# Taking the 64x64 inverse of a delta-rule block from a transpose on TensorE instead of from 32x32 products

## What is computed

```
sk = einsum('bhij,bhj->bhi', St, k_)
err = sk - v_
Sn = a_ * St - b_ * err[..., None] * k_[..., None, :]
o_ = einsum('bhij,bhj->bhi', Sn, q_)
```

## Time and profile before

| | us |
|---|---|
| median of 3 runs | 2829.43 (2828.09 to 2830.31) |
| the profiled execution | 2829.43 |
| its span | 2827.4 |
| TensorE busy | 2742.5 |
| VectorE busy | 1754.5 |
| ScalarE busy | 1222.6 |
| GpSimd busy | 607.1 |

### The profile page before, as it was taken

One profiled execution on the slowest core, in us unless ns is written; L12 is line 12 of the kernel. 1 busy time (PEld: TensorE's weight loads), 2 busy tenths in 40 slices (PEclk: granted clock), 3 DMA queues, 4 the chain that ended last, 5 costly groups with the idle time before them and its releaser, 6 DMA issues. The chain is left out here.

```text
span 2827.4 us, 38098 instructions
## 1 busy us (share of the span) xinstructions
PE 2742.5 (97%) x13297; PEld 1540.9 (54%) x13298; DVE 1754.5 (62%) x4334; ACT 1222.6 (43%) x2268; POOL 607.1 (21%) x670
## 2 busy tenths in 40 slices
PE   8999999989999988999999999999999999999998
PEld 3444444445566445665666656666566665664432
DVE  5867762011111176778877788777877778645986
ACT  4646441011211145456545565555645555342243
POOL 2111101401111312132133321333213331120000
PEclk9999999999999988999999999999999999999999
DMA  3101124031112562011100112001120011227313
GB/s 135 51 1 45 45 104 192 20 123 66 61 65 67 211 244 79 16 42 65 75 31 31 43 55 85 31 31 43 50 85 32 35 39 52 75 76 268 122 49 105
DMA packets 78503, 215.25 MB, mean 76 GB/s; under 512 B 12128, under 2 KB 13056, under 8 KB 69760
## 3 DMA queue, kind: packets, MB, share of 16 engines
q1 hardware_dynamic: 58704, 165.84, 16.2%
q0 software_dynamic: 9264, 28.36, 3.1%
q10 hardware_dynamic: 10368, 18.88, 1.8%
HBM read 156.25 MB, written 56.80 MB: 75 GB/s over the span
## 5 line engine op out<-in xcount | busy, mean ns | idle before, releaser
L2469 DVE SCALAR_TENSOR_TENSOR c_conv<-c_ps_pj,c_conv_t,c_conv 128x511 f32<-128x511 f32 (+2 forms) x450 | 336.0, 747 | 33.4 <-ACT c_conv L2288 22.8
L1962 POOL TENSOR_SCALAR c_gate<-c_gate 128x512 f32<-128x512 f32 x64 | 37.8, 618 | 980.5 <-DVE c_block_L L2502 980.5
L2038 PE MATMUL c_ps_pj<-c_xs,c_w_v 128*128 128x512 f32 x480 | 225.8, 593 | 0.0
L2038 PE MATMUL c_ps_pj<-c_xs,c_w_q 128*128 128x512 f32 x360 | 173.0, 610 | 0.0
L2059 PE MATMUL c_ps_pj<-c_w_g,c_xs 128*128 128x512 f32 x384 | 172.7, 592 | 0.0
L2038 PE MATMUL c_ps_pj<-c_xs,c_w_k 128*128 128x512 f32 x360 | 164.4, 593 | 0.0
L1284 DVE TENSOR_TENSOR x_act<-x_hs,x_ps_u 128x352 f32<-128x352 f32 x40 | 20.8, 521 | 191.5 <-ACT x_hs L1269 191.5
L2288 ACT ACTIVATE c_conv<-c_ps_pj,c_conv_t 128x512 f32<-128x512 f32 x150 | 116.3, 776 | 48.9 <-issue 27.4
L2351 ACT ACTIVATE c_err<-c_negL 32x128 f32<-32x128 f32 x256 | 78.6, 307 | 134.0 <-DVE c_negL L2535 129.3
L2499 DVE TENSOR_TENSOR c_block_X<-c_block_X,c_block_t 128x58 f32<-128x58 f32 (+6 forms) x448 | 117.7, 263 | 15.4
L2496 DVE TENSOR_TENSOR c_block_t<-c_block_L,c_block_X 128x58 f32<-128x58 f32 (+6 forms) x448 | 117.6, 262 | 14.9
(11 more groups left out here) (585 smaller groups left out, 5951.4 us busy)
## 6 DMA issues: line engine op xcount, KB each, us to landing
c_xs<-xt_d SPq DMA_DIRECT2D x16, 1024.0 KB, 4.8
c_G<-cum_d SPq DMA_DIRECT2D x16, 1024.0 KB, 4.7
ot_d<-c_oT ACTq DMA_DIRECT2D x64, 256.0 KB, 2.0
b_w_gu<-in_w_gu SPq DMA_DIRECT2D x8, 1408.0 KB, 21.5
y_slots<-x_y SPq DMA_DIRECT2D x40, 256.0 KB, 2.0
d_x<-x SPq DMA_DIRECT2D x32, 256.0 KB
d_switch<-in_switch_w SPq DMA_DIRECT2D x4, 2048.0 KB, 17.1
a_x<-in_x SPq DMA_DIRECT2D x7, 1024.0 KB, 7.3
```

The costliest lines, as they stand in the source:

```text
L2038: mm = e.matmul(bank_of[xb][u][:, :], w["kqv"[u // HG]][:, k, (u % HG) * DH:(u % HG + 1) * DH], xs[xb][:, k, :], start=(k == 0), stop=(k = ...
L2469: e.scalar_tensor_tensor(oc, bank_of[buf][u][:, 0:SEQ - s], conv_t[buf][:, m, h, TAPS - 1 - s:TAPS - s], oc, ALU.mult, ALU.add).then_inc(c ...
```

## The change

T's upper 64x64 is no longer put together from two spread blocks, a cleared block and a product. It is got in one piece as the transpose of R's upper 64x64, once that is whole.

- Gone: the 16 matmuls of L2167, T's spread 1 and the copy L2402 on ScalarE, and one clearing of a block of T on GpSimd at the phase's start.
- New on TensorE: `turn_inverse(p)`, eight transposes for each pair of chunks. The stationary operand is R's upper 64 rows by 128 columns, the moving one a 64x64 identity, so the output is 128 partitions by 64 columns, in `t_ps` for p = 0 and in `d_ps` for p = 1. They wait for both copies of R's off-diagonal blocks (`rl_done`, `rb_done`), for all spreads of R, and for the last copy of v (`v_done`), which `r_blocks` waited for before.
- New on ScalarE: two copies of 64x512, PSUM to T, behind the tap of unit HG+2.
- Order on TensorE: `r_blocks`, half of HG+2, **both `turn_inverse`**, half of HG+3, `z_half(0)`, a **quarter** of HG+3, `z_half(1)` with `r_half(0)`, the other **quarter**, `r_half(1)`. `z_half(p)` waits for the copy of T of its own pair.

```diff
-                e.memset(T[even_of[0], :, :, odd_of[0]], 0.0).then_inc(cleared, 1)
...
-                    e.wait_ge(T_done, 3 * r + 2)
+                    e.wait_ge(T_done, 2 * (r + 1))
...
-                    e.wait_ge(v_done, r * TPB + TPB)
...
-                            mm = e.matmul(t_block[odd_of[0], c, h, :], R[odd_of[0], c, h, odd_of[0]], Z[odd_of[0], c, h, even_of[0]],
-                                          start=True, stop=True)
-                            if c == TPB - 1 and h == HG - 1:
-                                mm.then_inc(tl_ready, 1)
...
+                def turn_inverse(p):
+
+                    if p == 0:
+                        e.wait_ge(v_done, r * TPB + TPB)
+                        e.wait_ge(R_done, TPB * r + TPB)
+                        e.wait_ge(rl_done, 3 * r + 1)
+                        e.wait_ge(rb_done, r + 1)
+                    for c in (2 * p, 2 * p + 1):
+                        for h in range(HG):
+                            mm = e.transpose(t_pair[p][:, c % 2, h, :], R[upper_half, c, h, :], con["ident"][upper_half, upper_half])
+                    mm.then_inc(tl_ready, 1)
+
+                def next_quarter(u, k):
+                    if not last:
+                        unit(r + 1, 1 - buf, u, (k // 2,), 16 * half + 16, ks=(k,))
+                        return
+                    h = (u + 1) * HG + k
+                    out_part(h // NH, (h % NH,))
...
-                    if i == 0 and p == 0:
-                        if not after_first(r):
-                            e.wait_ge(cleared, 3)
-                        e.wait_ge(T_done, 3 * r + 3)
-                        e.wait_ge(tl_done, r + 1)
+                    if i == 0:
+                        e.wait_ge(tl_done, PAIRS * r + p + 1)
...
                 next_unit(HG + 2, (1,))
+                for p in range(PAIRS):
+                    turn_inverse(p)
+                next_unit(HG + 3, (0,))
                 for i in range(2 * HG):
                     z_half(0, i)
-                next_unit(HG + 3, (0,))
+                next_quarter(HG + 3, 2)
                 for i in range(2 * HG):
                     z_half(1, i)
                     r_half(0, i)
-                next_unit(HG + 3, (1,))
+                next_quarter(HG + 3, 3)
...
-                spread(T, corner_T, 1, T_done)
                 next_silu(HG - 1)
-                e.wait_ge(tl_ready, r + 1)
-                e.activation(T[odd_of[0], :, :, even_of[0]], t_block[odd_of[0]], ACT.Copy).then_inc(tl_done, 1)
                 e.wait_ge(rl_ready, 4 * r + 2)
                 e.activation(R[even_of[1], :, :, odd_of[1]], r_block[1][even_of[1]], ACT.Copy).then_inc(rb_done, 1)
                 next_tap(HG + 2)
...
+                for p in range(PAIRS):
+                    e.wait_ge(tl_ready, PAIRS * r + p + 1)
+                    e.activation(T[upper_half, 2 * p:2 * p + 2, :, upper_half], t_pair[p][upper_half], ACT.Copy).then_inc(tl_done, 1)
```

More of the change, by code:

```diff
@@ L1802, in phase_delta @@
         z_block, r_block = [by_block(z_ps), by_block(d_ps)], [by_block(r_ps), by_block(kk_ps)]
-        t_block = by_block(t_ps)
-        z_pair, r_pair = [by_pair(z_ps), by_pair(d_ps)], [by_pair(r_ps), by_pair(kk_ps)]
+        z_pair, r_pair, t_pair = [by_pair(z_ps), by_pair(d_ps)], [by_pair(r_ps), by_pair(kk_ps)], [by_pair(t_ps), by_pair(d_ps)]
         even_of = [slice(2 * BB * b, 2 * BB * b + BB) for b in range(2)]
@@ L2190, in r_half @@
                     if i == 0:
[L2191 to L2194, removed]
                         e.wait_ge(zl_done, 4 * r + 3 + p)
```

## The result

The changed kernel took 2847.65 us in the median (2841.21 to 2849.38, 5 runs), the kernel before beside it 2828.39 us. The ratio of the means is 1.0062 with a 95% interval of 1.0047 to 1.0077: 0.6% slower, 17.5 us, with an interval of 13.3 to 21.8 us. The interval holds that, and it also holds the 20.9 us of the rival with 0.083 us per transpose: the total alone does not tell them apart, the rounds do. The profiled execution took 2848.35 us.

The account below looks back on a forecast made before the run. The prediction took TensorE to bound the kernel: 16 x 1.27 = 20.3 us added, 15 x 0.33 = 5.0 removed, r_blocks 0, so 2829.4 + 15.3 = 2844.7 us, range 2838 to 2857.

Parts of the forecast that it names:

- the rival with 0.083 us per transpose: New transposes take 0.083 us each, not 0.061: 2850.3 us in all; chance 0.13 together with the 0.109 case.
- TensorE sets the round: Attention rounds last as long as TensorE's work plus one wait of 0.3 us; TensorE time enters the span one to one.
- The third tile is free: In r_blocks, removing the 16 matmuls of L2167 saves 0.00 us, at most 0.01, since three tiles run side by side.
- The wait costs 0.33 us: First matmul of z_half(0) waits for ScalarE's copy of T; the new order removes 0.33 us in 15 rounds, 5.0 us.
- The turn block takes 1.27 us: The 16 new transposes on TensorE: 0.98 us plus 0.29 for changes of shape, in all 16 rounds, 20.3 us added.
- the slower-transpose rival: New transposes take 0.083 us each (2850.3 us) or 0.109 (2857.0 us), not 0.061; chance 0.13 for the two together.
- No new wait, thin cover: At r_half, a quarter of HG+3 covers ScalarE's copy of Z with 0.22 us margin, where 1.08 was; cost zero.
- The sum: Per execution: 20.3 us added, 5.0 removed, r_blocks 0; net +15.3 us, giving 2844.7 us, 0.5% slower.

Follow-up runs that it names:

- two_tiles: The kernel before without the 16 matmuls of L2167, ScalarE's copy waiting for the L2172 matmuls instead: ratio to before 0.9999.
- copy_first: The kernel before with ScalarE's copy of T (L2402) moved ahead of the silu: ratio to before 0.9982, 5.1 us faster.
- order_only: The kernel before with only the new TensorE order of HG+3's half and quarters, T made as before, no transposes: ratio to before 0.9980.
- no_cover: The changed kernel with both quarters of HG+3 ahead of z_half(1) and r_half(0), none ahead of r_half(1): ratio to before 1.0070.
- extra_turn: order_only plus 16 transposes of negL, result unused, ahead of the half of HG+3: ratio to before 1.0061.
- adjacent: order_only plus 16 transposes of negL, placed directly ahead of z_half(0): ratio to before 1.0048.

## Why the prediction was right

- *TensorE sets the round.* Right: the changed kernel's TensorE is busy for 89.89 of 89.89 us, and the turn block's 1.33 us less the wait's 0.33 are the 1.00 by which the round grew.
- *The third tile is free.* Right: 0.00 us in two_tiles. By a count of instructions the sum would have been 5.4 us smaller.
- *The wait costs 0.33 us.* Right: 88.89 to 88.56 in copy_first and order_only, 15 rounds, 5.0 us.
- *The turn block takes 1.27 us.* Right in kind, mis-sized by 0.06: it takes 1.33. The transpose was put at 0.061 and takes 0.0625; the changes of shape were put at 0.29, from the four transposes of L952, and take 0.33. That the 64 streamed and the 128 loaded columns would cost hardly more than either alone held. Neither the 0.083 nor the 0.109 of the slower-transpose rival is there. The loads of the new transposes, from the trace of the changed kernel, and those of the 128x128 ones, from that of the kernel before:

```profile
L2178 PEld LDWEIGHTS c_ps_t<-ident,c_R x128: 134/138/142, 1155.8 to 2512.4; 64*128 64x128 f32 x128
...
L2137 PEld LDWEIGHTS c_ps_t<-ident,c_vT x256: 139/141/142, 1129.4 to 2481.3; 128*128 128x128 f32 x128
```

  A load record lasts 138 ns here, 136 in L952 and 141 in the 128x128 transposes, though these stand 109 ns apart and the others 61 and 62.5. So the length of the record does not tell what a transpose costs, the distance between starts does. The 128 loaded columns are common to all three, so they don't set the 109; whether the 128 rows or the 128 streamed columns do, no run shows. The Trainium skill (TensorE: Matmul & The Clock Gate, LDWEIGHTS (loading the stationary operand)) gives a load of 128 columns 107 ns, by columns / 1.2. Neither the 62.5 ns between the new transposes nor the 138 ns of their load records agree with it.
- *No new wait, thin cover.* Right: the changed kernel has none, its margin is 0.23 us where 0.22 was forecast, and no_cover shows the wait that the quarter unit holds off.
- *The sum.* 16 x 1.33 - 15 x 0.33 = 16.3 us in place of 15.3. The two measurements, 17.5 and 14.4 us, lie on both sides of it. The profiled execution's other 2.6 us are 0.84 ahead of the first round's `z_blocks` and 1.74 of slower clock ahead of the last's. The forecast had no term for either; they are not the change's, and that the runs' scatter left the total near the forecast is luck in part.

So the change loses because it buys the end of a 0.33 us wait with a 1.33 us block, and what it saves on TensorE was never paid for. The wait could be had for nothing, by a swap of two lines on ScalarE.

## What to carry to other kernels

Count TensorE work by the distance between starts and not by instructions: here 16 matmuls of 32x32 hid under 32 others on other tiles of the array, while a new block of another shape paid its own way plus a third of a microsecond. Before paying for a wait with work, see whether the operation it waits for stands behind something on its own engine that nobody waits for. And where the bound engine has a fixed cadence, measure an edit by the length of a round in the trace, cut at the same instruction, which here repeats to 0.01 us, and not by total times that lie 9 us apart.

## What the runs showed of the hardware that was not expected

- The cost of a change of tile shape depends on the neighbour: 0.33 us for a block of 64x128 transposes between two units (extra_turn), 0.20 less where it borders on a 64x64 block (adjacent).
- A transpose with 64 rows, 128 loaded and 64 streamed columns of float32 takes 62.5 ns, little more than half of the 109 ns of a 128x128 one, though the load records last the same (138 and 141 ns).
- Behind the same wait of 3.3 to 3.5 us the granted clock stayed at 2.4 GHz in one trace of ten (1.00 over 7 us) and was at 1.2 GHz for a part in the others (0.77 over 6 us in the changed kernel's), where the next eight records took 1.4 to 3.0 us longer.
